# Second layer's experts: gate and up weights as the stationary operand, loaded for each tile into four slots

## The reference, cut to what matters

```python
# layer 1, for each token t and each of its 4 experts e (top 4 of sigmoid scores + e_bias)
gate, up = xn[t] @ w1[e], xn[t] @ w3[e]        # 192 each
y = (silu(gate) * up) @ w2[e]                  # 256
x[t] += tanh(g_ffn) * weight[t, e] * y         # the weights of a token sum to 1
```

## Time and profile before

| | us |
|---|---|
| median of 3 runs | 1429.08 (1428.9 to 1430.09) |
| the profiled execution | 1431.48 |
| its span, first to last instruction | 1429.7 |
| PE busy | 1149.8 (80%) |
| DVE busy | 713.6 (50%) |
| ACT busy | 594.3 (42%) |
| POOL busy | 319.1 (22%) |

### The profile page before, as it was taken

How to read it: one execution, slowest core, us unless ns; L and a number is a source line. 1 busy time by engine, 2 the same in 40 slices (tenths; PEclk the granted TensorE clock), 3 DMA queues, 4 the chain that set the end, 5 groups by cost and what they waited for, 6 DMA issues and landing times. The chain is left out here.

```text
span 1429.7 us, 25679 instructions
## 1 busy us (share of the span) xinstructions
PE 1149.8 (80%) x6415; PEld 712.2 (50%) x6416; DVE 713.6 (50%) x1862; ACT 594.3 (42%) x1386; POOL 319.1 (22%) x527
## 2 busy tenths in 40 slices
PE   3867999999943969999999999986548999999100
PEld 1667999999942512333233233324515777777000
DVE  4542222222226578888788788814392333333433
ACT  2451222222202515777777777772443333333000
POOL 2002222222115111111111111000004333332564
PEclk9956999999976968999999999998558999999655
DMA  9214555555516763113213213007302333333333
GB/s 298 84 58 148 181 183 183 183 183 180 171 64 199 258 134 48 25 23 49 32 16 47 32 16 47 1 1 193 109 1 85 99 103 100 100 101 95 99 109 101
DMA packets 94692, 147.95 MB, mean 103 GB/s; under 512 B 15398, under 2 KB 71616, under 8 KB 94490
## 3 DMA queue, kind: packets, MB, share of 16 engines
q1 hardware_dynamic: 78026, 103.74, 26.5%
q0 software_dynamic: 14288, 41.30, 9.6%
q10 hardware_dynamic: 2304, 2.10, 0.4%
HBM read 116.52 MB, written 30.38 MB: 103 GB/s over the span
## 5 line engine op out<-in xcount | busy, mean ns | idle before, releaser
L1894 DVE TENSOR_REDUCE arena<-ps 128x1 f32<-128x512 f32 x512 | 327.6, 682 | 66.8 <-PE ps L1735 60.0
L1865 ACT ACTIVATE arena<-ps 128x512 f32<-128x512 f32 (+1 forms) x576 | 303.5, 598 | 135.7 <-PE ps L1776 134.3
L1776 PE MATMUL ps<-arena 99*128 99x512 bf16 (+1 forms) x576 | 215.1, 386 | 6.2 <-ACT arena L1865 5.8
L1735 PE MATMUL ps<-arena 96*128 96x512 bf16 x512 | 204.7, 403 | 13.6 <-DMA arena<-k_parts 11.2
L863 POOL DMA_INDIRECT xg<-xn,tcol x134 | 127.7, 953 | 340.4 <-DVE tcol L896 336.6
L1765 PE MATMUL ps<-arena 128*17 128x512 f32 (+1 forms) x1152 | 151.6, 598 | 2.1 <-ACT arena L1865 1.0
L954 PEld LDWEIGHTS ps<-scratch,arena 128*128 128x128 f32 x1248 | 147.5, 194 | 3.6 <-issue 1.7
L954 PE MATMUL ps<-scratch,arena 128*128 128x128 f32 x1248 | 148.0, 278 | 1.1 <-ACT scratch L985 1.1
L1776 PEld LDWEIGHTS ps<-arena 99*128 99x128 bf16 (+1 forms) x576 | 56.8, 101 | 177.4 <-ACT arena L1865 141.8
L967 PE MATMUL ps<-arena,scratch 128*128 x624 | 141.0, 379 | 0.0
L1077 PE MATMUL ps<-arena,scratch 128*128 x380 | 139.6, 490 | 0.2 <-issue 0.2
(11 more groups left out here) (288 smaller groups left out, 1304.2 us busy)
## 6 DMA issues: line engine op xcount, KB each, us to landing
arena<-in_L_ffn_W SPq DMA_DIRECT2D x47, 1024.0 KB, 4.9
y<-ysb SPq DMA_DIRECT2D x95, 128.0 KB
arena<-in_L_ffn_w POOLq DMA_DIRECT2D x26, 384.0 KB, 10.1
arena<-in_L_ffn_w SPq DMA_DIRECT2D x44, 192.0 KB, 5.8
arena<-k_parts SPq DMA_DIRECT2D x48, 137.6 KB, 4.9
arena<-q_parts SPq DMA_DIRECT2D x96, 64.0 KB, 5.3
xn<-scratch SPq DMA_DIRECT2D x32, 128.0 KB, 1.7
scratch<-y SPq DMA_DIRECT2D x16, 256.0 KB, 2.9
```

What stands on the lines that cost most here:

```text
L1735: nc.tensor.matmul(ps[:, MAXB + pos % NMAXB, :], e.q_aug[u][0:QROWS, c, h, t * P:(t + 1) * P], e.k_aug[u][0:QROWS, h, CL + k * HB:CL + (k ...
L1776: nc.tensor.matmul(ps[0:rows, SB + n % NSB, :], e.k_aug[u][0:AROWS, h, k0:k0 + rows], e.q_aug[u][0:AROWS, c, h, :], start=True, stop=True) ...
L1865: nc.scalar.activation(e.prob[s % 2][0:rows, h, :], ps[0:rows, SB + (s * GH + h) % NSB, :], ACT.Exp).then_inc(p_ready, 1)
L1894: v.tensor_reduce(e.mx[:, c, h, t, k:k + 1], ps[:, MAXB + pos % NMAXB, :], AX.X, ALU.max).then_inc(max_done, 1)
```

## The change

In `experts1`, W1 and W3 become the stationary operand: three pieces of 128 columns of the joined 384, two matmuls each, with the 128 columns of `xT` moving. The result then has hidden features on partitions, so `turn_hidden` and the copy behind it (`copy_hidden`) are gone. The hidden part is 192 = 128 + 64 rows (IA, IB) in place of 96 + 96, ACT takes the silu in two instructions (128 and 64 partitions), DVE multiplies in three of 64 partitions each, and they write `hT`, which `down` reads directly.

W1 and W3 are no longer resident. SP reads each tile's expert into a register and loads its W1 and W3 by two DMAs of 192 KB into one of four slots; the load of tile j waits until `gate_up(j-4)` is done (`gu_raw`), and PE's `gate_up(j)` waits for the slot's semaphore. The same queue stores y, six tiles behind the loads. W2 takes 16 DMAs, which POOL issues during `project_qkv` in place of its 26 for W1 and W3. The blocks of SP in `project_out` and `route` of layer 1 are removed.

```diff
-W2_1 = E1 * W13_BYTES
-ARENA = W2_1 + E1 * 2 * D * 4
+W2_1 = 0
+W13_1 = W2_1 + E1 * 2 * D * 4
+W2_TURN = 4
+ARENA = 163840
 E1_SCRATCH = 2 * 4 * D * 4
 LOGITS_AT = 3 * 4 * D * 4
 TOP = ARENA - (DK * D + D + DK * E1) * 4
-W2_TOP = (TOP - W2_1) // (2 * D * 4)
-EARLY = 26
-ATT0 = EARLY * W13_BYTES
+ATT0 = W13_1 + RING1 * W13_BYTES
+IA, IB = P, I1 - P
...
-    e.w13 = carve(0, [E1, DK, 2 * I1])
     e.w2b = carve(W2_1, [E1, 2, D])
+    e.w13 = carve(W13_1, [RING1, DK, 2 * I1])
...
-        if layer == 1:
-            @block.sync
-            def _(sp):
-                for x in range(W2_TOP, E1):
-                    load_w2(e, sp, x)
...
+    w13_in = [sem(f"e1_w13_in{r}") for r in range(RING1)]
     x_turned, xT_ready = sem("e1_x_turned"), sem("e1_xT_ready")
-    gu_raw, silu_ready, a_ready, a_turned, aT_ready = (sem("e1_" + n) for n in ("gu_raw", "silu_ready", "a_ready", "a_turned", "aT_ready"))
+    gu_raw, silu_ready, h_ready = sem("e1_gu_raw"), sem("e1_silu_ready"), sem("e1_h_ready")
     y_raw, y_ready, tcol_ready = sem("e1_y_raw"), sem("e1_y_ready"), sem("e1_tcol_ready")
     y_stored = [sem(f"e1_y_stored{r}") for r in range(RING1)]
     o = 0
     xT = e.carve(o, [2, DK, P], base=e.scr); o += 2 * DK * P * 4
-    silu = e.carve(o, [2, I1], base=e.scr); o += 2 * I1 * 4
-    act_in = e.carve(o, [2, I1], base=e.scr); o += 2 * I1 * 4
-    aT = e.carve(o, [2, 2, P], base=e.scr); o += 2 * 2 * P * 4
+    silu = e.carve(o, [2, 2, P], base=e.scr); o += 2 * 2 * P * 4
+    hT = e.carve(o, [2, 2, P], base=e.scr); o += 2 * 2 * P * 4
     assert o <= E1_SCRATCH
-    XB, GB, TB, YB = 0, 2, 4, 6
+    XB, GB, UB, YB = 0, 2, 4, 6
+    LAG_Y = RING1 + 2
+    def chunk(r, n):
+        return ps[:, GB + r % 2, 0:P] if n == 0 else ps[:, UB + r % 2, (n - 1) * P:n * P]
...
+        @block.sync
+        def _(sp):
+            def load(j, r):
+                ex = sp.value_load(e.expert[0:1, bass.ds(j, 1)], min_val=0, max_val=E1 - 1)
+                if at_least(j, RING1):
+                    sp.wait_ge(gu_raw, (j - RING1) * 2 + 2)
+                for at, name in ((0, "L1_ffn_w1"), (I1, "L1_ffn_w3")):
+                    sp.dma_start(e.w13[:, r, :, at:at + I1], e.a[name][bass.ds(ex, 1)].rearrange("e (k p) i -> p (e k) i", p=P)).then_inc(w13_in[r], 16)
+            def store(j, r):
+                sp.wait_ge(y_ready, j + 1)
+                sp.dma_start(e.y[1][bass.ds(j * P, P), :], e.ysb[:, r, :]).then_inc(y_stored[r], 16)
+            def body(j, r, turn, first, last):
+                load(j, r)
+                if at_least(j, LAG_Y):
+                    store(j - LAG_Y, (r - LAG_Y) % RING1)
+            for j in range(LAG_Y):
+                load(j, j % RING1)
+            turns = (NT1 - LAG_Y) // RING1
+            with sp.Fori(0, turns) as t:
+                for u in range(RING1):
+                    body(t * RING1 + (LAG_Y + u), (LAG_Y + u) % RING1, None, False, False)
+            for j in range(LAG_Y + turns * RING1, NT1):
+                body(j, j % RING1, None, False, False)
+            for j in range(NT1 - LAG_Y, NT1):
+                store(j, j % RING1)
+            for r in range(RING1):
+                sp.wait_ge(y_stored[r], 16 * ((NT1 - 1 - r) // RING1 + 1))
...
-            def gate_up(j, r, ex):
+            def gate_up(j, r, turn):
+                pe.wait_ge(w13_in[r], turn * 32 + 32)
                 pe.wait_ge(xT_ready, j + 1)
-                for k in range(DK):
-                    ins = nc.tensor.matmul(ps[:, GB + r % 2, 0:2 * I1], xT[:, r % 2, k, :], e.w13[:, ex, k, :], start=(k == 0), stop=(k == DK - 1))
-                ins.then_inc(gu_raw, 1)
-            def turn_hidden(j, r):
-                pe.wait_ge(a_ready, j + 1)
-                for k in range(2):
-                    ins = nc.tensor.transpose(ps[0:IH, TB + r % 2, k * P:(k + 1) * P], act_in[:, r % 2, k * IH:(k + 1) * IH], e.ident[:])
-                ins.then_inc(a_turned, 1)
+                for n in range(3):
+                    for k in range(DK):
+                        ins = nc.tensor.matmul(chunk(r, n), e.w13[:, r, k, n * P:(n + 1) * P], xT[:, r % 2, k, :], start=(k == 0), stop=(k == DK - 1))
+                    if n != 1:
+                        ins.then_inc(gu_raw, 1)
             def down(j, r):
-                ex = expert(j)
+                ex = pe.value_load(e.expert[0:1, bass.ds(j, 1)], min_val=0, max_val=E1 - 1)
                 if at_least(j, 2):
                     pe.wait_ge(y_ready, j - 1)
-                pe.wait_ge(aT_ready, j + 1)
-                for k in range(2):
-                    last = nc.tensor.matmul(ps[:, YB + r % 2, 0:D], aT[0:IH, r % 2, k, :], e.w2b[0:IH, ex, k, :], start=(k == 0), stop=(k == 1))
+                pe.wait_ge(h_ready, j + 1)
+                for k, rows in enumerate((IA, IB)):
+                    last = nc.tensor.matmul(ps[:, YB + r % 2, 0:D], hT[0:rows, r % 2, k, :], e.w2b[0:rows, ex, k, :], start=(k == 0), stop=(k == 1))
                 last.then_inc(y_raw, 1)
-            def expert(j):
-                return pe.value_load(e.expert[0:1, bass.ds(j, 1)], min_val=0, max_val=E1 - 1)
             def body(j, r, turn, first, last):
-                gate_up(j, r, expert(j))
-                if at_least(j, 1):
-                    turn_hidden(j - 1, (r - 1) % RING1)
+                if at_least(j, 2):
+                    pe.wait_ge(h_ready, j - 1)
+                gate_up(j, r, turn)
                 if isinstance(j, int) and j == 2:
-                    pe.wait_ge(e.w2_in, 16 * E1)
+                    pe.wait_ge(e.w2_in, 32 * (E1 // W2_TURN))
                 if at_least(j, 2):
                     down(j - 2, (r - 2) % RING1)
                 if before(j, NT1 - 2):
...
             for j in range(2):
                 turn_x(j, j, 0)
-            pe.wait_ge(e.w13_early, 32 * EARLY // 2)
-            pe.wait_ge(e.w13_in, 32 * (E1 - EARLY))
...
+                if at_least(j, 2):
+                    act.wait_ge(gu_raw, (j - 2) * 2 + 2)
                 nc.scalar.activation(xT[:, r % 2].rearrange("p k t -> p (k t)"), ps[:, XB + r % 2, 0:D], ACT.Copy).then_inc(xT_ready, 1)
-            def copy_hidden(j, r):
-                act.wait_ge(a_turned, j + 1)
+            def body(j, r, turn, first, last):
                 if at_least(j, 2):
-                    act.wait_ge(y_raw, j - 1)
-                nc.scalar.activation(aT[0:IH, r % 2].rearrange("p k t -> p (k t)"), ps[0:IH, TB + r % 2, 0:2 * P], ACT.Copy).then_inc(aT_ready, 1)
-            def body(j, r, turn, first, last):
-                act.wait_ge(gu_raw, j + 1)
-                if at_least(j, 2):
-                    act.wait_ge(a_ready, j - 1)
-                nc.scalar.activation(silu[:, r % 2], ps[:, GB + r % 2, 0:I1], ACT.Silu).then_inc(silu_ready, 1)
-                if at_least(j, 1):
-                    copy_hidden(j - 1, (r - 1) % RING1)
+                    act.wait_ge(h_ready, j - 1)
+                act.wait_ge(gu_raw, j * 2 + 1)
+                nc.scalar.activation(silu[:, r % 2, 0, :], chunk(r, 0), ACT.Silu).then_inc(silu_ready, 1)
+                act.wait_ge(gu_raw, j * 2 + 2)
+                nc.scalar.activation(silu[0:IB, r % 2, 1, :], chunk(r, 1)[0:IB], ACT.Silu).then_inc(silu_ready, 1)
                 if before(j, NT1 - 2):
...
-                dve.wait_ge(silu_ready, j + 1)
+                dve.wait_ge(silu_ready, j * 2 + 2)
                 if at_least(j, 2):
-                    dve.wait_ge(a_turned, j - 1)
-                v.tensor_tensor(act_in[:, r % 2], ps[:, GB + r % 2, I1:2 * I1], silu[:, r % 2], ALU.mult).then_inc(a_ready, 1)
+                    dve.wait_ge(y_raw, j - 1)
+                v.tensor_tensor(hT[0:IB, r % 2, 0, :], chunk(r, 1)[IB:P], silu[0:IB, r % 2, 0, :], ALU.mult)
+                v.tensor_tensor(hT[IB:P, r % 2, 0, :], chunk(r, 2)[0:IB], silu[IB:P, r % 2, 0, :], ALU.mult)
+                v.tensor_tensor(hT[0:IB, r % 2, 1, :], chunk(r, 2)[IB:P], silu[0:IB, r % 2, 1, :], ALU.mult).then_inc(h_ready, 1)
...
-            for ex in range(0, EARLY, 2):
-                load_w13(e, pool, ex, e.w13_early, 2)
+            for ex in range(0, E1, W2_TURN):
+                load_w2(e, pool, ex)
...
-    eng.dma_start(e.w2b[0:IH, ex, :, :], e.a["L1_ffn_w2"][ex].rearrange("(k p) d -> p k d", p=IH)).then_inc(e.w2_in, 16)
-
-def load_w13(e, eng, ex, loaded, n=1):
-    for at, name in ((0, "L1_ffn_w1"), (I1, "L1_ffn_w3")):
-        eng.dma_start(e.w13[:, ex:ex + n, :, at:at + I1], e.a[name][ex:ex + n].rearrange("e (k p) i -> p e k i", p=P)).then_inc(loaded, 16)
-
+    w = e.a["L1_ffn_w2"][ex:ex + W2_TURN]
+    eng.dma_start(e.w2b[0:IA, ex:ex + W2_TURN, 0, :], w[:, 0:IA].rearrange("e p d -> p e d")).then_inc(e.w2_in, 16)
+    eng.dma_start(e.w2b[0:IB, ex:ex + W2_TURN, 1, :], w[:, IA:I1].rearrange("e p d -> p e d")).then_inc(e.w2_in, 16)
...
-        @block.sync
-        def _(sp):
-            for ex in range(EARLY, E1):
-                load_w13(e, sp, ex, e.w13_in)
-            for ex in range(W2_TOP):
```

(16 more changed lines are left out.)

## The result

| | us |
|---|---|
| median of the changed kernel, 5 runs | 1437.86 (1435.49 to 1439.3) |
| median of the kernel before, 5 runs | 1428.9 (1425.67 to 1430.09) |
| ratio | 1.0074, 95% interval 1.0055 to 1.0093 |
| the profiled execution, its span | 1435.79, 1434.0 |

The change is slower, by 0.7% or 10.6 us (7.9 to 13.3), where 20.9 us less were forecast. It lies outside the range of 1403 to 1420.

What follows compares the result with a forecast made beforehand. PE's instructions in `experts1` were taken as the bound, with SP's issuing at the end of `project_out` second. -16.2 - 4.7 = -20.9 us gave 1410.6 on the profile's scale, a median of 1408.2; range 1403 to 1420.

Steps and rivals of the forecast that it cites:

- PE in experts1: PE's tile in `experts1` goes from 2.60 to 2.43 us, -16.2 us over 95 tiles, if PE stays the bound.
- The rival on weight loads: In `experts1`, eight more weight loads of 0.194 us a tile aren't hidden: +122, 1551 us; chance 0.02.
- `gate_up`: In PE's tile of `experts1`, twelve instructions of 0.1117 us take 1.34 us against 1.29: +0.05.
- `turn_hidden` and its copy: In `experts1`, `turn_hidden` goes from PE's tile, -0.22 us; a copy goes from ACT, whose time stays about the same.
- `project_out`: At its end, the wait for SP's 42 issues goes; the router starts at 997.3 in place of 1002.05, -4.7 us.
- the clock in the router: PE's clock in the router is half and expected to stay low; otherwise the router could save up to 3 us.
- `project_qkv` at nothing: There, 26 issues become 16, 3.7 MB less; taken as 0, between -1.3 and +1 us.
- The start of `experts1` at nothing: First weights land about 1077.2, before PE's first `gate_up` at 1078.88, the fourth before tile 3; no cost.
- SP's turn: SP's queue in `experts1`: expert read, two load issues, store and steps take 2.28 us a tile, under PE's 2.43.
- the first rival: SP or a part-filled transfer sets the pace in `experts1`: SP 2.48 to 2.55 us a tile, 1416.8 to 1420; chance 0.16.
- Slots and transfers: In `experts1`, weights reach the four slots in time; transfers take 2.13 of 2.43 us a tile, 88% full.
- DVE's three multiplies: In `experts1`, three multiplies of 64 x 128 at 0.344 us each; DVE 1.51 us a tile against 2.43.

Runs made afterwards that it cites:

- experiments 1 and 2: `a_pad128` and `a_pad96`: the changed kernel with `down`'s second matmul padded with zeros to 128 and 96 rows; 1429.63 and 1426.16 us.
- `a_pad96`: The changed kernel with `down`'s second matmul on 96 rows in place of 64, 32 of them zeros; 1426.16 us, one run.
- `a_pad128`: The changed kernel with `down`'s second matmul on 128 rows in place of 64, 64 of them zeros; 1429.63 us, ratio 0.9956 to the kernel before.

## Why the prediction was wrong

- **The step that failed** is in "PE in experts1": "`down` has 128 and 64 rows in place of 96 and 96, and I give that nothing, since what lasts there is the 256 moving columns". It measured +0.34 us a tile (`down` 0.87 to 1.16, `turn_x` 0.22 to 0.27), 95 x 0.34 = 32 us. The tile became 2.77 in place of 2.43. No row of the trace before had a 64-row matmul in this stage, so the term had no basis; it should have been bounded like the others. A 64-row load left in the open would have been 2 x 0.19 us, and with this the sum is about +15: a slower case of real weight. The rival on weight loads looked at the eight new loads of 128 rows, which are hidden, and not at the two whose shape was new.
- **`gate_up`** as 12 x 0.1117: right, 1.34 us.
- **`turn_hidden` and its copy** gone: right, 0.22 us, shown by the 2.43 of experiments 1 and 2.
- **`project_out`** -4.7: right, the gap went from 5.11 to 0.30 us; the clock in the router stayed low, also as forecast. `project_qkv` at nothing: nothing seen of it (from its first matmul to `attend`'s 71.5 us before, 71.1 after). The start of `experts1` at nothing: W1 and W3 were there in time, as forecast, but the first gather landed later, +1.1.
- **SP's turn** at 2.28 us: too small, and hidden by the first error. It measured 2.59, because the turns without a loop end are about 2.4 (the read of the expert and its steps were taken from layer 0's first two) and the end of a loop of four, which the sum left out, adds about 0.6 (3.03 against 2.44, the mean of the three others). With the rows cured SP is the bound: the first rival, only at 2.59 where it was given 2.48 to 2.55. The forecast would still have been some 16 us too good, since in `a_pad96` the stage took 249.3 us against 250.5, so -1.2 + 1.1 - 4.8 = -4.9 in place of -20.9 (`a_pad128` measured a ratio of 0.9956, which is -6.3, between -10.0 and -2.7).
- **Slots and transfers** were right for the kernel as it ran: PE has no wait on W1 or W3, and the share is 0.83. DVE's three multiplies took 0.29 us each, less than the 0.344 they were priced at.

## What to carry to other kernels

Price every matmul whose number of rows the change alters, and look at its neighbours: a piece of 64 rows between pieces of 128 costs a change of height on either side, and rows of zeros up to 96 or 128 cost PE nothing. When a stage is bound by one engine, add up the next one's queue with its loop's end too: here SP at 2.59 us a tile stood right behind PE's 2.43, and a store given to an engine with room was worth 7.5 us of the stage (249.3 to 241.8). An instruction that is neither added nor removed can still get dearer, so compare start with next start for all parts of a tile.

## What the hardware did that I had not expected

- A weight load behind a change from 128 to 64 rows or back begins only some 0.31 us behind the start of the matmul ahead: 310, 320, 306 and 166 ns between starts in place of 216, 220, 215 and 111; at 96 rows (with 128 beside it) there is no such cost.
- Matmuls of 64 rows on the lower and the upper half of the rows start 6 ns apart and run side by side.
- The end of SP's loop of four tiles costs it about 0.6 us (3.03 against 2.33 to 2.60 for a turn), that of eight tiles 0.26 (2.65 against 2.39). Why they differ isn't known.
- `combine` lasted 92.6 and 102.4 us, and `attend` 457.5 and 465.3, in two profiles of the same kernel.
